# The first product of a graph kernel: x loaded in chunks of four row tiles, and the norms of the four early tiles in one chain

## The reference

```python
h = jnp.maximum(_layernorm(x, axis=-1), 0.0)      # rows of x: mean, variance, 1/sqrt, relu
x = x + _L0_gnn_ref(h, adj, adj)
# _L0_gnn_ref(x=h, Coefficient2=adj, A=adj):
#   S = (A + A.T) * 0.5
#   adj1 = S + eye;  deg = sum(adj1, axis=1);  dinv = where(deg > 0, deg ** -0.5, 0)
#   adj2 = dinv[:, None] * adj1 * dinv[None, :]
#   return (Coefficient2 @ adj2) @ h
h = jnp.maximum(_layernorm(x, axis=-1), 0.0)
x = x + _L1_gnn_ref(h, adj, W, a1, a2, W1, b1, ...)   # 8 heads of attention, then four dense layers
```

## Time and profile before

| | |
|---|---|
| median of 3 runs | 918.83 us (916.86 to 919.87) |
| the profiled execution, its own time | 916.54 us |
| its span | 914.6 us |
| busy share of the span | PE 94%, DVE 76%, ACT 45%, POOL 30% |
| granted PE clock, mean | 0.985 |
| instructions | 15458 |

### The profile page before, as it was taken

How to read it: one execution, slowest core, us unless ns; L and a number is a source line. 1 busy time by engine, 2 the same in 40 slices (tenths; PEclk the granted TensorE clock), 3 DMA queues, 4 the chain that set the end, 5 groups by cost and what they waited for, 6 DMA issues and landing times.

```text
span 914.6 us, 15458 instructions
## 1 busy us (share of the span) xinstructions
PE 859.8 (94%) x5144; PEld 753.6 (82%) x5144; DVE 691.7 (76%) x1199; ACT 412.0 (45%) x743; POOL 275.2 (30%) x287
## 2 busy tenths in 40 slices
PE   1899999989999999999599999999999999998997
PEld 1687888868888888778399999999999999997553
DVE  5688886554556875666899999999999999997622
ACT  2344433221212111245386666666666656774331
POOL 0000000000000000057646555555555545573111
PEclk9999999998999999999799999999999999999999
DMA  9949930009332222130051000000000022001132
GB/s 344 406 168 301 395 132 1 0 20 292 126 104 100 92 92 69 58 127 4 27 199 25 23 23 24 25 24 23 24 24 24 23 93 70 13 1 47 47 136 96
DMA packets 36131, 87.36 MB, mean 96 GB/s; under 512 B 7088, under 2 KB 7984, under 8 KB 36080
## 3 DMA queue, kind: packets, MB, share of 16 engines
q1 hardware_dynamic: 35040, 82.46, 26.2%
q0 software_dynamic: 1040, 4.26, 1.2%
HBM read 73.93 MB, written 12.78 MB: 95 GB/s over the span
## 4 chain that ended last, share of the span: by engine, by line
PE 45%; DVE 3%; POOL 1%; ACT 1%; issue 1%; ACTq 0%; POOLq 0%; DVEq 0%
PE bank L1593 24%; PE bank L1617 13%; PE bank L2046 3%; DVE l_q L1278 2%; PE bank L73 1%; PE bank L74 1%; PE bank L75 1%; PE bank L2029 1%; PE bank L2038 1%; PE bank L2008 1%; DVE wh L1959 0%; POOL l_parts L1512 0%; POOL l_o_q L1505 0%; ACT l_mask L1391 0%; POOL l_o_m L1524 0%
## 5 line engine op out<-in xcount | busy, mean ns | idle before, releaser
L1278 DVE SCALAR_TENSOR_TENSOR l_q<-bank,neg_d,mask 128x512 fp32r<-128x512 f32 x512 | 338.6, 741 | 28.3 <-PE bank L1593 27.4
L1593 PE MATMUL bank<-l_parts,l_q 128*128 128x260 f32 x2048 | 250.7, 284 | 8.3 <-DVE l_q L1278 8.3
L1593 PEld LDWEIGHTS bank<-l_parts,l_q 128*128 128x128 f32 x2048 | 248.3, 189 | 8.4 <-issue 8.4
L838 POOL TENSOR_TENSOR l_prod<-wh,l_a 128x512 f32<-128x512 f32 x30 | 36.6, 1239 | 407.2 <-ACT wh L808 406.4
L1391 ACT ACTIVATE l_mask<-mask 128x512 fp32r (+1 forms) x256 | 136.3, 619 | 0.2
L1617 PE MATMUL bank<-l_parts,l_mask 128*128 128x260 f32 x1024 | 129.0, 286 | 2.0 <-ACT l_o_q L1397 2.0
L1617 PEld LDWEIGHTS bank<-l_parts,l_mask 128*128 128x128 f32 x1024 | 127.1, 189 | 2.3 <-ACT l_o_q L1397 2.2
L73 PE MATMUL bank<-l_g_hi,l_a_hi 128*128 128x512 f32 x256 | 100.8, 394 | 4.5 <-DVE l_a_lo L856 4.2
L74 PE MATMUL bank<-l_g_lo,l_a_hi 128*128 128x512 f32 x256 | 100.6, 393 | 0.0
L75 PE MATMUL bank<-l_g_hi,l_a_lo 128*128 128x512 f32 x256 | 100.4, 392 | 0.0
L783 ACT ACTIVATE l_a_hi<-rows 128x1024 fp32r<-128x1024 f32 x32 | 33.9, 1062 | 147.2 <-PE bank L75 124.6
(11 more groups left out here) (176 smaller groups left out, 1241.1 us busy)
## 6 DMA issues: line engine op xcount, KB each, us to landing
rows<-adj_t SPq DMA_DIRECT2D x48, 512.0 KB, 4.1
l_now<-adj SPq DMA_DIRECT2D x16, 512.0 KB, 7.6
l_rows_k<-adj_t SPq DMA_DIRECT2D x16, 512.0 KB, 8.5
l_src<-e_rows SPq DMA_DIRECT2D x30, 256.0 KB, 3.2
l_kept<-adj SPq DMA_DIRECT2D x12, 512.0 KB, 12.7
wh_store<-wh POOLq DMA_DIRECT2D x1, 4160.0 KB, 14.3
x<-x SPq DMA_DIRECT2D x1, 4096.0 KB, 14.2
x_store<-x SPq DMA_DIRECT2D x1, 4096.0 KB, 12.8
```

Of the source, the lines that this page charges most:

```text
L838: p.tensor_tensor(per_head(prod[:, b, n, :]), wh[:, t, :, 0:HD], per_head(a_b[:, n, :]), ALU.mult).then_inc(prod_ready, 1)
L1278: v.scalar_tensor_tensor(out=q[:, i, :], in0=bank[S_BANKS[hh]][:], scalar=neg_d[:, i, h:h + 1], in1=mask[:, i, cols], op0=ALU.is_ge, op1=A ...
L1593: return pe.matmul(bank[Q_BANKS[hh][t]][:, 0:PW], q[:, i, t * P:(t + 1) * P], parts[pair_slot][:, hh, i, :], start=i == 0, stop=i == T - 1)
```

## The change

Chunks of x are all four tiles long. SP issues x for tiles 0 to 3 first, in one DMA, and then the loads of tiles 0 to 5; x for tiles 4 to 7 follows where it did. DVE runs one chain of norms for the four early tiles before anything else, and after it does all that tile i needs for tiles 0, 1 and 2 in one fixed order, ending in `cut_x_lo(i)`; ACT normalises four tiles at first. What was interleaved (the norms of tiles 2 and 3, the sums of tile 3) is so in sequence. From tile 4 on only the numbers of the chunks differ.

```diff
-        CHUNKS = ((0, 2), (2, 4), (4, 8), (8, 12), (12, 16))
+        CHUNKS = ((0, 4), (4, 8), (8, 12), (12, 16))
...
                 load_x(0)
-                load(0)
-                load(1)
+                for i in range(EARLY + 2):
+                    load(i)
                 load_x(1)
-                for i in range(2, EARLY + 2):
-                    load(i)
-                load_x(2)
                 load(EARLY + 2)
                 load(EARLY + 3)
+                load_x(2)
                 load_x(3)
-                load_x(4)
...
                 variances(0)
                 for n in range(6):
                     refine(0, n)
-                add_now(0)
-                add_kept(0)
-                degree(0)
-                guard(0)
-                cut_lo(0)
-                invert(0)
-                square(0)
-                correct(0)
-                scale(0)
-                add_now(1)
-                cut_x_lo(0)
-                add_kept(1)
-                degree(1)
-                statistics(1)
-                guard(1)
-                variances(1)
-                cut_lo(1)
-                invert(1)
-                refine(1, 0)
-                square(1)
-                refine(1, 1)
-                correct(1)
-                refine(1, 2)
-                scale(1)
-                refine(1, 3)
-                add_now(2)
-                cut_x_lo(1)
-                refine(1, 4)
-                add_kept(2)
-                refine(1, 5)
-                degree(2)
+                for i in range(3):
+                    add_now(i)
+                    add_kept(i)
+                    degree(i)
+                    guard(i)
+                    cut_lo(i)
+                    invert(i)
+                    square(i)
+                    correct(i)
+                    scale(i)
+                    cut_x_lo(i)
                 add_now(3)
-                guard(2)
-                cut_lo(2)
-                invert(2)
                 add_kept(3)
-                square(2)
                 degree(3)
-                correct(2)
                 guard(3)
-                scale(2)
                 invert(3)
                 square(3)
-                cut_x_lo(2)
                 correct(3)
+                scale(3)
                 cut_lo(3)
-                scale(3)
+                cut_x_lo(3)
                 add_now(4)
-                cut_x_lo(3)
                 cut_lo(4)
                 add_kept(4)
                 degree(4)
-                statistics(2)
+                statistics(1)
...
                 take_ln_root(0)
-                normalise(0, 0, 2)
-                a.wait_ge(summed, 1)
-                cut_hi(0)
-                take_root(0)
-                cut_x_hi(0)
-                a.wait_ge(summed, 3)
-                cut_hi(1)
-                take_root(1)
-                take_ln_root(1)
-                cut_x_hi(1)
-                normalise(1, 2, 4)
+                normalise(0, 0, 4)
+                for i in range(2):
+                    a.wait_ge(summed, 2 * i + 1)
+                    cut_hi(i)
+                    take_root(i)
+                    cut_x_hi(i)
                 take_root(2)
                 cut_hi(2)
+                cut_x_hi(2)
                 take_root(3)
-                cut_x_hi(2)
                 cut_hi(3)
                 cut_x_hi(3)
                 cut_hi(4)
```

More of the change, by code:

```diff
@@ L405, in _ @@
                 degree(4)
-                statistics(2)
+                statistics(1)
                 guard(4)
-                variances(2)
+                variances(1)
                 cut_lo(5)
@@ L411, in _ @@
                 invert(4)
-                refine(2, 0)
+                refine(1, 0)
                 add_kept(5)
                 square(4)
-                refine(2, 1)
+                refine(1, 1)
                 degree(5)
                 correct(4)
-                refine(2, 2)
+                refine(1, 2)
                 guard(5)
                 scale(4)
-                refine(2, 3)
+                refine(1, 3)
                 cut_lo(6)
-                refine(2, 4)
+                refine(1, 4)
                 add_now(6)
-                refine(2, 5)
+                refine(1, 5)
                 invert(5)
@@ L443, in _ @@
                 cut_x_lo(8)
-                statistics(3)
+                statistics(2)
                 invert(7)
-                variances(3)
+                variances(2)
                 square(7)
@@ L451, in _ @@
                 scale(7)
+                refine(2, 0)
+                statistics(3)
+                refine(2, 1)
+                variances(3)
+                refine(2, 2)
+                cut_lo(10)
+                refine(2, 3)
+                cut_x_lo(10)
+                refine(2, 4)
                 refine(3, 0)
-                statistics(4)
+                add_now(8)
+                refine(2, 5)
                 refine(3, 1)
-                variances(4)
+                add_kept(8)
                 refine(3, 2)
-                cut_lo(10)
+                degree(8)
                 refine(3, 3)
-                cut_x_lo(10)
+                guard(8)
                 refine(3, 4)
-                refine(4, 0)
-                add_now(8)
+                cut_lo(11)
                 refine(3, 5)
[L464 to L472, removed]
                 cut_x_lo(11)
@@ L579, in _ @@
                 take_root(4)
-                take_ln_root(2)
+                take_ln_root(1)
                 cut_hi(5)
@@ L583, in _ @@
                 cut_hi(6)
-                normalise(2, 4, 6)
+                normalise(1, 4, 6)
                 take_root(6)
                 cut_hi(7)
-                normalise(2, 6, 8)
+                normalise(1, 6, 8)
                 take_root(7)
@@ L590, in _ @@
                 cut_x_hi(8)
-                take_ln_root(3)
+                take_ln_root(2)
                 cut_hi(9)
                 cut_x_hi(9)
-                take_ln_root(4)
+                take_ln_root(3)
                 cut_hi(10)
                 cut_x_hi(10)
-                normalise(3, 8, 10)
+                normalise(2, 8, 10)
                 take_root(8)
@@ L600, in _ @@
                 cut_x_hi(11)
-                normalise(3, 10, 12)
+                normalise(2, 10, 12)
                 for i in range(9, T):
@@ L606, in _ @@
                     if i < 13:
-                        normalise(4, i + 3, i + 4)
+                        normalise(3, i + 3, i + 4)
                 for s in range(FIRST_LATE - 1, STEPS):
```

## The result

The changed kernel took 912.57 us (median of 5, 911.92 to 913.76) against 916.86 for the kernel before on the same chip: a ratio of 0.9947, 95% interval 0.9931 to 0.9964. Two later comparisons on other occasions gave 0.9948 (0.9931 to 0.9964) and 0.9953 (0.9934 to 0.9972). Forecast was 5.2 us less and a median of 913.6. The ratio makes it 4.9 less (3.3 to 6.3 by its interval); the two medians lie 4.3 apart. The median of the kernel before was 918.83 in the three runs that the forecast started from and 916.86 in five, so a part of the distance between 913.6 and 912.57 is the choice of the base. The profiled execution took 911.92 us with a span of 910.0; forecast was 911.3 and 909.4.

What follows compares the result with a forecast made beforehand. PE was taken as the bound from step 3 on, held up before by waits for cut_x_lo. Step 3 earlier by 4.9 us plus 0.3 from later waits made 5.2: 918.83 to 913.6 us, range 911.0 to 916.5.

Steps and rivals of the forecast that it cites:

- What bounds: From step 3 on PE is the bound; a microsecond that step 3 starts earlier is one off the end.
- First DMA: Twice the bytes: x used at 5.8 us, all behind it up to x's former place lands 1.25 us later.
- Norms and ACT: DVE's norms of four tiles done at 10.0, ACT's normalising at 13.1; added work hidden by added DMA time.
- Steps 0 to 3: PE's first steps: starts at 17.9, 25.5, 31.9 and 37.7; step 3 comes 4.9 us earlier.
- The clock: Idleness of 0.9 us ahead of step 2 leaves full clock, which saves 1.7 us in step 2.
- Supply of steps 4 to 11: DVE and ACT chain 5.2 us earlier, statistics at 41.2; a third of a microsecond of later waits goes.
- A: Clock still falls to 1.2 GHz in step 2: gain 4.2, 914.6 us; chance 0.16 together with D.
- C: Slower: DVE waits at 41.2 for x of tiles 4 to 7; landing at 48 gives 920.2 us; chance 0.04.
- D: cut_x_lo(2) still late through ACT because x lands late: gain 3.0, 915.8 us; chance 0.16 together with A.
- B: Loads of tiles 11 to 15, between 86 and 118 us, give it back: gain 1 or less, 918; chance 0.08.

Runs made afterwards that it cites:

- Theory 2's first kernel: Changed kernel with root, invert, square, correct and scale ahead of cut_lo for tiles 0 to 2, as for tile 3: 0.9953 of the kernel before.
- The kernel with the chunks alone: Changed kernel with four-tile chunks and one chain of norms kept, but sums and cuts of tiles 0 to 3 in the old order: 0.9979 of the kernel before.
- Theory 2's two kernels: Changed kernel with tiles 0 to 2 in tile 3's order; the second also loads x for tiles 4 to 7 before tile 5: 0.9953, 0.9937 of the kernel before.
- the eight operations: Changed kernel with eight extra bn_stats on DVE between guard(2) and cut_lo(2): 1.0024 of the kernel before, 0.9993 when run once more.

## Why the prediction was right, step by step

*What bounds.* Right: PE behind step 3, and a microsecond at step 2 is one at the end (1.12 in, 1.11 out). Toward earlier starts this ends at the supply of steps 4 to 11: the 2.2 us of Theory 2's first kernel gave 0.4.

*First DMA.* x came at 6.15 (forecast 5.8; bounds 5.4 and 8.4). The prediction also works out a gain of 4.3 by the Trainium skill ("DMA: Bandwidth & Descriptors", section "Bandwidth"), with x near 6.9. Here, on another kind of queue, that is too late: the DMA of 1 MB was in 5.4 us after its issue at 0.76.

The shift of all behind it by 1.25 us was wrong. Tile 0's second half was in by 11.72, not 12.6, and at 11.9 to 12.1 in traces where a wait shows it. For tile 1 DVE's row at 17.94 has no wait for a DMA and tells only that its data were in. The kernel with the chunks alone waits for them, and they come at 17.06:

```profile
17.06 1.23 DVE L305 SCALAR_TENSOR_TENSOR l_now<-rows,l_now 128x1024 f32<-128x1024 f32 x1 [0.58 <-DMA l_kept<-adj]
```

Theory 2's two kernels have 17.34 and 17.27, so the shift is 0.5 to 0.8, and tile 3, for which I had no shift, came 0.87 earlier there. What failed is the one rate for all: 417 GB/s was read between 10 and 15 us, but the bytes in question move earlier, where the kernel before had 236 GB/s from 4 to 6 us and the changed one 411. Windows of 2 us summed up to 12 us give the changed kernel 0.17 MB more, so my estimate from them is that the 0.52 MB set back what lies behind them by 0.35 MB, 0.8 us. That x for tiles 2 and 3 had landed at 17.85 was a coincidence.

*Norms and ACT.* DVE was done at 10.5, ACT at 13.4, 0.3 to 0.5 later than forecast, for the most part by x's delay. Since tile 0's data came sooner than forecast, ACT's added work was not hidden behind them: DVE stood idle for 1.03 us for `cut_hi(0)`, and `cut_lo(0)` began at 14.48 (14.25), step 0 at 18.17 (17.9).

*Steps 0 to 3.* Step 0 had eleven slow matmuls (ten before) and took some 7.9 us, and so the idleness ahead of step 2 shrank to 0.27 by the row, 0.4 counted from start to start, where I had 0.9. In two more traces it was none (13 slow matmuls) and 0.80 by the row (8), and step 2 began at 31.98 and 31.94, so step 0 was worth next to nothing, as forecast. The prediction reads the low level in step 0 from the granted clock; the clock's column has 1.00 there, and what shows the level is the spacing: 0.43 us from start to start, as in step 2 at a clock of 0.50, against 0.23. This is the window over step 0 in the changed kernel:

```profile
18.00:23.00 5.00, 4.83 (x12) 3.84 (x13) 4.54 (x13) 1.51 (x3) 0.00 (x0) 1.00 1.02 407
```

The start of step 2, 31.9, was exact, since it hangs on DVE: `cut_lo(2)` 28.2 forecast, 28.21 measured; `cut_x_lo(2)` at 31.0 both times. Luck has a part in that. DVE has no wait for a DMA between 14.48 and 28.21, so its delay of 0.2 to 0.3 us at `cut_x_lo(0)` went through, and it was made up by the wait for tile 1 that I had put at 17.85 and that was not there: without it my sum would have had `add_now(1)` at 17.7. Step 3: 37.7 forecast, 37.73 measured.

*The clock.* No fall in step 2, as forecast, and the 1.7 us that I gave it, less the 0.4 of the new wait, are the 1.3 of the eight operations. But one inference was weak. I took the idle 1.95 us at 386.36 as proof that such a gap is harmless, by the first matmul behind it, which took 0.50 us. That matmul doesn't tell: in step 2 of the kernel before the first one took 0.47, and the matmuls of 0.62 us began 1.2 us behind it. There was indeed no fall at 386.36 (clock 1.00 up to 398 us). In the changed kernel the same gap, at 380.40, did bring the low clock:

```profile
380.40 0.50 PE L73 MATMUL bank<-l_w_hi,l_g_hi 128*128 128x512 f32 x1 [1.95 <-DVE l_g_lo L880]
```

```profile
382.00:384.00 2.00, 2.00 (x7) 1.52 (x6) 1.33 (x3) 0.00 (x0) 0.00 (x0) 0.50 1.04 390
```

One trace without a fall was not enough for a rule: of the 13 traces of this case the same gap of 1.95 us brought the low clock in five. That 0.9 was far below it carried the forecast.

*Supply of steps 4 to 11.* The statistics were due at 41.2 and ran at 41.28, by DVE's own chain: their x was issued at 23.81, not 24.57, and landed near 40.5, not 41.2. The 0.7 us of later waits became 0.4, and the stretch from step 3 to the mark 0.27 shorter, where I had 0.3. The sum for the first product, 5.2, measured 5.16.

*The rivals.* A (the clock falls in step 2) and C (x for tiles 4 to 7 holds DVE) are refuted by the rows above; D's late `cut_x_lo(2)` too. B (later stages give it back) did not hold: the loads of tiles 11 to 15 moved with PE, since product and steps end 5.16 earlier. Yet the profiled span shrank by 4.6, not 5.2. From the second product to the end the changed kernel's trace is 0.6 us longer: it has a fall behind the 1.95 us of idleness (1.6 us more) and one near 829 us (1.2 more), the one before has a fall 15 us behind that idleness instead (1.6), and its stretch up to that idleness is 0.8 longer. The next section shows how such things differ between executions.

## What to carry to other kernels

In a sequence written out by hand, look for an instruction that waits for a late input (here the sum of tile 3) ahead of one whose inputs are all there (the cuts of tile 2). Here swapping them was worth 4.9 us, and saving operations together with the merged DMA 0.3 to 0.85. Price idleness of PE with the clock that follows it, and rest no rule for that on one trace. Follow the next engine's chain past the gap: after the swap, the DMA of x for tiles 4 to 7 was the next limit, only 0.8 us away. Ask of each time that comes out right whether the row shows a wait: a start without one tells only that its data were in. Judge a change of half a per cent by a mark in the trace at the end of the changed stage, and only then by whole times.

## What the runs showed of the hardware

Idle times of PE of 1.74 and 1.79 us ahead of step 2 left the clock at 1.00; 2.88, 3.59, 4.29 and 4.45 brought 0.50 for some 3 us, and 3.90 ahead of the second product brought it in all 13 traces of this case. At 1.95, in a later stage, both were seen: the low clock in five of the 13, and the stretch up to the next such idle time then took 15.8 us instead of 14.2. The Trainium skill ("TensorE: Matmul & The Clock Gate", Part 1) says that the number of slow matmuls differs from run to run of one kernel; step 0 agrees: eleven of them in the changed kernel's first trace, 13 and 8 in two more.

A second thing differs from execution to execution, and it is no clock. In three traces of the changed kernel the second product began at 200.56, 200.58 and 200.79, but the spans were 910.0, 912.9 and 912.9: 2.9 us between the first two arise behind the changed stage, with the work the same. The stretch from the second product to the matmul behind the 1.95 us of idleness took 179.84 us in one (200.56 to 380.40) and 181.77 in the other (200.58 to 382.35). The clock is low for the same 3.4 us in both. What differs is one wait of PE, 24 to 26 us behind the mark, 0.24 us long in the first trace and 2.14 in the second:

```profile
226.37 0.47 PE L73 MATMUL bank<-l_g_hi,l_a_hi 128*128 128x512 f32 x1 [2.14 <-DVE l_a_lo L821]
```

It goes back through DVE and ACT to a DMA of rows of the transpose, for which ACT waited up to 223.90 instead of 221.97. The kernel with eight operations more has a wait of 1.40 there in one trace and none in the other, and with a fall at the 1.95 us in the first one only, these two make 2.9 of the 3.0 us by which its traces differ behind the mark. So in these two pairs of executions falls of the clock and the landing of this DMA make most of the difference; the scatter of the other runs was not followed. Why that DMA lands at different times is open.
